# One-hot rows of relation and node: made by GpSimd behind its gathers instead of by VectorE

## What is computed

```python
def step(m, rw):
    r, w_r = rw
    mask = jnp.where(etypes == r, 1.0, 0.0).astype(h.dtype)
    m = m + mask[:, None] * (h @ w_r)          # h = feat[src]
    return (m, None)
m, _ = jax.lax.scan(step, m0, (jnp.arange(n_rels), weight))
out = jax.ops.segment_sum(m, dst, num_segments=feat.shape[0])
...
x = _layernorm(x + out, axis=-1)
```

## Time and profile before

| what | us |
|---|---|
| time, median of 3 runs | 767.06 |
| lowest and highest of the runs | 766.12, 768.82 |
| profiled execution, first to last instruction (its own time) | 1331.0 |
| TensorE matmuls busy in the profiled execution | 905.4 (68%) |
| VectorE busy | 656.1 (49%) |
| ScalarE busy | 628.9 (47%) |
| GpSimd busy | 553.1 (42%) |

### The profile page before, as it was taken

The page is one execution under the profiler, slowest core; times in us unless marked ns, Lnnn a source line. Parts: engine busy times, 40 slices in busy tenths (PEclk is TensorE's granted clock), DMA queues, the critical chain, the costliest instruction groups (busy, mean ns, idle before and its releaser), DMA issues.

```text
span 1331.0 us, 25286 instructions
## 1 busy us (share of the span) xinstructions
PE 905.4 (68%) x8746; PEld 801.7 (60%) x8747; DVE 656.1 (49%) x2201; ACT 628.9 (47%) x1217; POOL 553.1 (42%) x591
## 2 busy tenths in 40 slices
PE   4576686766766768676675857667676766767676
PEld 3465575665656657566565756557575655756575
DVE  7653644545545364453635445363544545354444
ACT  6455453553544535444453535445363444535442
POOL 5643534444434353343534344352533435344341
PEclk9687887877868688686887778786787778788676
DMA  6211211111111111111111111121111111111111
GB/s 166 54 45 37 53 40 39 42 46 42 43 36 46 33 51 42 38 45 34 49 40 41 38 41 43 34 51 28 53 41 36 45 34 51 35 44 43 28 28 35
DMA packets 29901, 58.93 MB, mean 44 GB/s; under 512 B 11656, under 2 KB 11906, under 8 KB 29882
## 3 DMA queue, kind: packets, MB, share of 16 engines
q0 software_dynamic: 18464, 37.85, 11.0%
q1 hardware_dynamic: 11264, 20.41, 5.8%
q10 hardware_dynamic: 154, 0.42, 0.1%
HBM read 56.23 MB, written 2.40 MB: 44 GB/s over the span
## 4 chain that ended last, share of the span: by engine, by line
PE 66%; issue 30%; ACT 2%; DVE 1%; DMA 0%; ACTq 0%; DVEq 0%
PE own L767 48%; PE agg L805 11%; PE rel L818 6%; ACT pick L426 1%; DVE outT L647 0%; DMA x_sb<-in_x 0%; ACT away L420 0%; PE rel L825 0%; PE own L915 0%; DVE x_sb L681 0%; ACT rows L436 0%; DVE xp L558 0%; PE own L748 0%; ACT idx L451 0%; DVE outT L622 0%
## 5 line engine op out<-in xcount | busy, mean ns | idle before, releaser
L767 PE MATMUL own<-xp,pick 125*128 125x192 bf16 x5725 | 653.5, 271 | 377.6 <-issue 371.3
L767 PEld LDWEIGHTS own<-xp,pick 125*128 125x128 bf16 x5725 | 545.9, 108 | 474.6 <-issue 458.6
L345 POOL DMA_INDIRECT rows<-x_parts,gidx x558 | 529.5, 949 | 612.5 <-ACT gidx L379 231.1
L539 DVE TENSOR_SCALAR pick<-src_h,node 125x516 bf16<-125x516 f16 (+1 forms) x1220 | 459.7, 456 | 291.5 <-ACT src_h L387 290.3
L435 ACT ACTIVATE rows<-own 128x384 bf16<-128x384 f32 x122 | 57.4, 470 | 643.0 <-remote 581.2
L622 DVE TENSOR_TENSOR outT<-outT,rel 64x32 f32 x124 | 22.3, 180 | 361.6 <-PE rel L825 349.2
L420 ACT ACTIVATE away<-src_h,node_neg 125x516 bf16<-125x516 f16 (+1 forms) x305 | 192.5, 693 | 7.6 <-PE own L767 5.9
L426 ACT ACTIVATE pick<-away,one 125x516 bf16<-125x516 bf16 (+1 forms) x305 | 192.0, 696 | 0.0
L805 PE MATMUL agg<-onehot,rows 128*128 128x112 bf16 x2418 | 167.9, 243 | 15.8 <-issue 15.6
L805 PEld LDWEIGHTS agg<-onehot,rows 128*128 128x128 bf16 x2418 | 163.7, 117 | 18.3 <-issue 18.1
L605 DVE TENSOR_SCALAR onehot<-ramp,krel 128x112 bf16<-128x112 bf16 x806 | 148.9, 262 | 6.6 <-PE agg L805 6.6
(11 more groups left out here) (67 smaller groups left out, 83.0 us busy)
## 6 DMA issues: line engine op xcount, KB each, us to landing
src_b<-in_src SPq DMA_DIRECT2D x61, 258.0 KB
rows<-x_parts,gidx POOLq DMA_INDIRECT x577
x_parts<-xp SPq DMA_DIRECT2D x1, 728.0 KB
x_parts<-xp SPq DMA_DIRECT2D x1, 672.0 KB
out<-x_sb SPq DMA_DIRECT2D x2, 224.0 KB
x_sb<-in_x ACTq DMA_DIRECT2D x1, 364.0 KB
x_sb<-in_x SPq DMA_DIRECT2D x1, 336.0 KB
src_i<-in_src SPq DMA_DIRECT2D x1, 312.0 KB
```

The costliest lines, as they stand in the source:

```text
L345: pool.indirect_dma_start(rows[:, u, j, :], None, x_parts, bass.IndirectOffsetOnAxis(ap=gidx[:, u, j:j + 1], axis=0)).then_inc(rows_in[u] ...
L539: v.tensor_scalar(pick[u][:, b, 0:CUT * cut_width(u, odd)], src_h[u][:, :, 0:cut_width(u, odd)], node[:, b:b + 1], None, ALU.is_equal).the ...
L767: return nc.tensor.matmul(own_slot(u, h), pick[u][:, b, h * P:(h + 1) * P], xp[:, b, 0:SPLIT, :].rearrange("p s d -> p (s d)"), start=(b = ...
```

## The change

GpSimd makes the one-hot blocks of every group from turn 1 on: 60 groups of 13, 780 instructions. They stand between its gathers, one or two behind each (behind the nine gathers of a group 1, 1, 2, 1, 2, 1, 2, 1, 2). The scalar is read from a new small buffer `gkrel`, 13 keys a group, which ScalarE copies out of `krel` right behind its copy of the indices, when the marks of the group before in that buffer are done. VectorE makes the 26 blocks of turn 0 only. `onehot_ready[u]` is now incremented by GpSimd's last mark of a group. The helpers `gather` and `mark` are new names for what one DMA and one one-hot block issue.

```diff
+        gkrel = sb("gkrel", [P, 2, GT])
...
+            def mark(u, j):
+
+                return pool.tensor_scalar(onehot[:, u, j, :], ramp[:, :, 0:R], gkrel[:, u, j:j + 1], None, ALU.is_equal)
...
+                marked = 0
                 for j in range(OWN[u], GT):
-                    pool.indirect_dma_start(
-                        rows[:, u, j, :], None, x_parts,
-                        bass.IndirectOffsetOnAxis(ap=gidx[:, u, j:j + 1], axis=0)).then_inc(rows_in[u] if j < LATE else late_in[u], 16)
+                    gather(rows_in[u] if j < LATE else late_in[u], u, j)
+                    if is_first(i):
+                        continue
+                    if j == OWN[u]:
+                        pool.wait_ge(gkrel_ready[u], i)
+                        pool.nop(nofuse=True)
+                    n = GT if j == GT - 1 else (j + 1 - OWN[u]) * GT // (GT - OWN[u])
+                    for m in range(marked, n):
+                        last = mark(u, m)
+                    marked = n
+                if not is_first(i):
+                    last.then_inc(onehot_ready[u], 1)
...
                 act.activation(gidx[:, u, :], idx[:, bass.ds(i * (2 * GT) + u * GT, GT)], ACT.Copy).then_inc(gidx_ready[u], 1)
+                if not is_first(i):
+                    if not (isinstance(i, int) and i == 1):
+                        act.wait_ge(onehot_ready[u], i)
+                    act.activation(gkrel[:, u, :], krel[:, bass.ds(i * (2 * GT) + u * GT, GT)], ACT.Copy).then_inc(gkrel_ready[u], 1)
...
             def onehots(i, u):
 
-                if not is_first(i):
-                    dve.wait_ge(agg_ready[u], i)
...
                 if not is_first(i):
-                    onehots(i, 1)
-                if not is_first(i):
                     add_rel(i - 1)
                 if more:
                     picks(i + 1, 1, not odd)
-                    onehots(i + 1, 0)
```

More of the change, by code:

```diff
@@ L171, in gnn_resnorm @@
         xT_done, xT_taken = sem("xT_done"), sem("xT_taken")
+        gkrel_ready = sem2("gkrel_ready")
         gidx_ready, rows_in, late_in = sem2("gidx_ready"), sem2("rows_in"), sem2("late_in")
@@ L328, in _, with gather @@
             pool.wait_ge(parts_out, 64)
+            def gather(s, u, j):
+                pool.indirect_dma_start(
+                    rows[:, u, j, :], None, x_parts,
+                    bass.IndirectOffsetOnAxis(ap=gidx[:, u, j:j + 1], axis=0)).then_inc(s, 16)
+            def mark(u, j):
+                return pool.tensor_scalar(onehot[:, u, j, :], ramp[:, :, 0:R], gkrel[:, u, j:j + 1], None, ALU.is_equal)
             def fetch(i, u, odd):
@@ L336, in fetch @@
                     for j in range(FEWER):
-                        pool.indirect_dma_start(
-                            rows[:, u, j, :], None, x_parts,
-                            bass.IndirectOffsetOnAxis(ap=gidx[:, u, j:j + 1], axis=0)).then_inc(first_in, 16)
+                        gather(first_in, u, j)
                 if own_count(u, odd) == FEWER:
-                    pool.indirect_dma_start(
-                        rows[:, u, FEWER, :], None, x_parts,
-                        bass.IndirectOffsetOnAxis(ap=gidx[:, u, FEWER:FEWER + 1], axis=0)).then_inc(fourth_in, 16)
+                    gather(fourth_in, u, FEWER)
+                marked = 0
                 for j in range(OWN[u], GT):
-                    pool.indirect_dma_start(
-                        rows[:, u, j, :], None, x_parts,
-                        bass.IndirectOffsetOnAxis(ap=gidx[:, u, j:j + 1], axis=0)).then_inc(rows_in[u] if j < LATE else late_in[u], 16)
+                    gather(rows_in[u] if j < LATE else late_in[u], u, j)
[10 more added lines that the diff above has]
+                    last.then_inc(onehot_ready[u], 1)
             def turn(i, odd):
```

## The result

| kernel | median us | runs |
|---|---|---|
| before | 767.94 | 4, from 766.12 to 769.04 |
| after | 1207.28 | 4, from 1206.02 to 1207.69 |

The ratio is 1.5725, 95% interval 1.57 to 1.5751: 439 us slower, where 203 were forecast. The sign was right, the size less than half, and the time lies above the range.

What follows compares the result with a forecast made beforehand. GpSimd's queue was taken as the bound, its floor 764.6 us against 767.06 timed; 780 marks at 0.26 us add 203 us, everything else nothing, giving 970 us. The range was 795 to 1050 us.

Steps and rivals of the forecast that it cites:

- GpSimd sets the time, and every mark counts in full: GpSimd's queue has no room, so 780 marks at 0.26 us add 203 us to 767.06.
- The floor of 1.25 us a gather: GpSimd's 577 gathers back to back, with start and end, sum to 764.6 us, 2.5 under the timed median.
- Rival 2: Recording stretches GpSimd too; a timed gather is 0.95 us: 797 us (chance 0.08), or no change, 767 us (0.05).
- rival 3: Faster: VectorE's 144 us are freed, gaps and marks on GpSimd are cheap, TensorE bounds at about 730 us; chance 0.07.
- The price of a mark: One one-hot instruction on GpSimd: 0.26 us from its rows at the start, ends 0.185 and 0.36 us.
- The Trainium skill's price: About 1.8 cycles an element at 1.2 GHz on GpSimd: 168 ns a mark without dispatch, +131 us in sum.
- The gap: The 0.30 us between GpSimd's gathers is part of a gather's own work, so marks cannot hide in it.
- rival 1: Marks fill the 0.30 us between gathers; only pairs overhang, by 0.2 us, 48 us in all: 815 us; chance 0.13.
- Rival 4: Each mark opens its own 0.30 us before the next gather, 162 us more: 1132 us; chance 0.06.
- What VectorE gains: VectorE loses 780 one-hots, 144 us of busy time, none on the path: gain nothing.
- The profiled span: The recorded span after the change should stay within 3% of 1331.0 us, paced by a stretched TensorE.
- TensorE's floor: TensorE's own instructions back to back: 712 us, or about 730 with its small transposes.

Runs made afterwards that it cites:

- The later recording: The kernel before, recorded again with no edit: 766.71 us, span 764.8 us.
- the half dose: Against the kernel after, GpSimd makes only the marks of u = 0 (390) and VectorE those of u = 1 as before: 986.49 us.
- the copies: Against the kernel after, each mark is a plain copy of the ramp to the one-hot block, key and compare left out: 915.31 us.

## Why the prediction was wrong, step by step

- **GpSimd sets the time, and every mark counts in full: right.** The floor of 1.25 us a gather met the later recording (764.8 us of span), the half dose came out at 986.49 for 987, and thirty gathers fewer gave time back. A mark with a window of 0.581 us adds 0.563. Rival 2 and rival 3 fall with it.
- **The price of a mark: the step that failed.** I took 0.26 us from GpSimd's rows of other instructions, and for the upper end CAST's 1.06 ns a column twice over, 0.36. Measured 0.563: 0.286 of columns at 2.55 ns, 0.20 fixed, 0.078 for the key. These rows do price the window of a copy (0.28 us), but a tensor-scalar instruction runs its columns 2.4 times as slowly as CAST, and no row of the trace had one on GpSimd. The whole miss is 780 x 0.303 = 236 us, and 970 + 236 = 1206. An upper end drawn from another instruction's row was no bound.
- **The Trainium skill's price.** The Trainium skill (GPSIMD Engine Reference, section 3.1) led to an estimate of 168 ns for the columns, by the pace that it calls the best case; the runs show 286. Its advice in section 4.1 to leave elementwise work to VectorE is borne out: 185 ns there against 563.
- **The gap: right that a mark can't hide in it, wrong that it is a fixed price.** In front of a gather behind a mark it is 0.17 us, not 0.30, while the gather is 1.03 instead of 0.94. So for a mark the two nearly cancel, and rival 1 falls, but a shorter instruction does go into the gap in part: the copies, 0.28 us each, add 148 us (915.31), not 780 x 0.28 = 218. Adding whole windows was a second error of the sum, of the other sign, and the price hid it. Rival 4's 1132 us lay nearest to the result, with a mechanism that did not occur.
- **What VectorE gains: right, nothing.** Its busy time fell by 140 us (656.1 to 516.4; 144 were forecast). ScalarE's copies, 60 of 201 ns, and its wait cost nothing on the path.
- **The profiled span: wrong.** I expected 1331 us again and found 1205.8. The reason I gave, recording, was wrong too; it did no harm to the sum because the sum was made by floors and not from the stretched span.
- **TensorE's floor: too low.** 712 to 730 were estimated from its matmuls back to back; with its waits for picks its side stands at 744.5 us.

## What to carry to other kernels

Before work is moved to an engine, add up that engine's instructions with the time from one start to the next, not its busy share: GpSimd at 72% was full, and its 42% was a share of an odd execution. A price taken from another kind of instruction is a guess, and its upper end should say so; where the queue is full and hundreds of instructions go into it, one run with the instruction alone in the old kernel is worth more than any row. A profile whose span is far from the timed runs is best recorded again before anything is explained from it.

## What the runs showed of the hardware

- A gather of 128 rows of 512 bytes holds GpSimd's queue for 1.25 us behind another gather, 0.94 recorded as busy and 0.30 not.
- A tensor-scalar instruction on GpSimd costs 2.5 ns a column from 64 to 1456 columns, whether it compares or subtracts, from bf16 or fp32, dense or in pieces; a scalar read a partition adds 0.078 us. A copy of the same 112 columns adds 0.189 us between gathers.
- The marks take 581 ns beside an idle VectorE and 580 under its instructions.
- With a loop body of four turns instead of two TensorE's branch back took 3.7 to 3.9 us instead of 0.21 to 0.25, and instructions were fetched all through the loop, 82 packets from 200 to 700 us against none.
